# Two transformer layers on one core: the stores of the results are asked for by ScalarE's queue instead of SyncE's

## The reference

```python
def _L0_cond_ref(x, t_emb, W_ada, b_ada, Wq, Wkd, Wku, Wvu, Wo):
    ...
    scores = jnp.where(mask[None, None], jnp.asarray(-jnp.inf, x.dtype), scores)
    attn = jax.nn.softmax(scores, axis=-1)
    y = jnp.einsum('bhts,bhsd->bhtd', attn, v_exp)
    out = y.transpose(0, 2, 1, 3).reshape(B, T, C) @ Wo.T
    return x + out
def _L1_cond_ref(x, pos_ids, time_emb, ln1_w, ln1_tw, ln2_w, ln2_tw, Wq, Wk, Wv, Wo, Wg, Wu, Wd):
    ...
    x = res + ctx @ Wo.T
    res = x
    h = ada_rms(x, time_emb, ln2_w, ln2_tw)
    mlp = jax.nn.silu(h @ Wg.T) * (h @ Wu.T) @ Wd.T
    return res + mlp
```

## Time and profile before

| what | us |
|---|---|
| median of three executions | 1815.69 |
| the profiled execution | 1816.14 |
| its span | 1814.2 |
| PE busy | 1713.0 |
| DVE busy | 1155.3 |
| ACT busy | 945.1 |
| POOL busy | 398.2 |

### The profile page before, as it was taken

How to read it: one execution, slowest core, us unless ns; L and a number is a source line. 1 busy time by engine, 2 the same in 40 slices (tenths; PEclk the granted TensorE clock), 3 DMA queues, 4 the chain that set the end, 5 groups by cost and what they waited for, 6 DMA issues and landing times.

```text
span 1814.2 us, 37803 instructions
## 1 busy us (share of the span) xinstructions
PE 1713.0 (94%) x12416; PEld 929.7 (51%) x12416; DVE 1155.3 (64%) x2956; ACT 945.1 (52%) x2775; POOL 398.2 (22%) x554
## 2 busy tenths in 40 slices
PE   6586888999999999999999999999999999999999
PEld 2244444565455545555455554555455554555444
DVE  6768566585677657685576756676576855767320
ACT  3836456364664537554483646645385644835320
POOL 3448477011110211111110111111121111101120
PEclk9786999999999999999999999999999999999999
DMA  7867489472794448662594637843495626936220
GB/s 244 149 183 117 126 187 241 102 129 74 157 187 88 83 111 186 139 115 80 126 193 91 119 84 163 172 96 76 120 191 124 122 73 139 194 88 108 99 70 23
DMA packets 527236, 234.38 MB, mean 129 GB/s; under 512 B 476336, under 2 KB 493744, under 8 KB 527024
## 3 DMA queue, kind: packets, MB, share of 16 engines
q1 hardware_dynamic: 511472, 175.09, 48.8%
q10 hardware_dynamic: 15552, 56.63, 9.9%
HBM read 90.09 MB, written 16.78 MB: 59 GB/s over the span
## 4 chain that ended last, share of the span: by engine, by line
PE 77%; DVE 9%; DMA 6%; issue 4%; ACT 3%; SPq 1%; DVEq 0%; POOL 0%; ACTq 0%
PE up L1395 8%; PE up L1397 8%; PE up L1396 8%; PE gate L1395 7%; PE gate L1397 7%; PE gate L1396 7%; DMA prob_t<-prob 5%; PE bank L1395 4%; PE y L1395 4%; PE y L1397 4%; PE bank L1396 4%; PE y L1396 4%; PE bank L1397 4%; PE bank L1422 2%; PE bank L1459 1%
## 5 line engine op out<-in xcount | busy, mean ns | idle before, releaser
L843 ACT ACTIVATE bank<-bank,low 128x128 f32<-128x128 f32 (+2 forms) x768 | 302.7, 395 | 63.4 <-DVE low L1079 36.7
L685 POOL TENSOR_TENSOR inner_t<-inner,inner_t 128x512 f16<-128x512 f32 x128 | 149.0, 1164 | 665.6 <-ACT inner_t L1022 665.6
L1086 DVE TENSOR_TENSOR prob<-bank,prob 128x512 f16<-128x512 f32 (+1 forms) x320 | 202.8, 634 | 57.1 <-ACT prob L852 55.9
L852 ACT ACTIVATE prob<-bank 128x512 f16<-128x512 f32 (+1 forms) x320 | 178.7, 558 | 75.4 <-DMA prob_t<-prob 52.7
L1395 PE MATMUL up<-mlp,ring 128*128 128x512 f16 x512 | 195.2, 381 | 13.3 <-DVE inner L1360 13.3
L1350 DVE SCALAR_TENSOR_TENSOR silu<-silu,gate 128x512 f32<-128x512 f32 x128 | 87.9, 687 | 181.4 <-ACT silu L1016 180.5
L1395 PE MATMUL gate<-mlp,ring 128*128 128x512 f16 x512 | 194.7, 380 | 1.4 <-DVE mlp L1055 0.9
L1397 PE MATMUL up<-mlp,ring 128*128 128x512 f16 x512 | 195.2, 381 | 0.0
L1396 PE MATMUL up<-mlp,ring 128*128 128x512 f16 x512 | 195.2, 381 | 0.0
L1396 PE MATMUL gate<-mlp,ring 128*128 128x512 f16 x512 | 194.5, 380 | 0.0
L1397 PE MATMUL gate<-mlp,ring 128*128 128x512 f16 x512 | 194.5, 380 | 0.0
(11 more groups left out here) (176 smaller groups left out, 4020.7 us busy)
## 6 DMA issues: line engine op xcount, KB each, us to landing
ring<-wgu_dram ACTq DMA_DIRECT2D x108, 512.0 KB, 3.8
x_in<-x_dram SPq DMA_DIRECT2D x18, 512.0 KB, 3.8
x_res<-x_mid SPq DMA_DIRECT2D x16, 512.0 KB, 4.9
wgu_dram<-ring SPq DMA_DIRECT2D x16, 512.0 KB, 3.6
out_dram<-x_res SPq DMA_DIRECT2D x32, 256.0 KB, 2.4
prob_t<-prob SPq DMA_TRANSPOSE x256, 3.6
inner_t<-wd_t_dram SPq DMA_DIRECT2D x4, 1024.0 KB, 8.7
ring<-wg_t_dram SPq DMA_DIRECT2D x16, 256.0 KB, 4.0
```

What stands on the lines that cost most here:

```text
L685: pool.tensor_tensor(inner_t[:, 1, f, :], inner[:], inner_t[:, 0, f, :], ALU.subtract).then_inc(inner_low, 1)
L843: ins = act.activation(bank_[:, at:at + wid], bank_[:, at:at + wid], ACT.Exp, bias=low[:, j % BANKS, k:k + 1], scale=-1.0, accum_out=total)
L852: act.activation(terms(prob[:, g % SLOTS, 0, :], layer, j), terms(work_bank[USE[f"unit{layer}", j] % BANKS][:], layer, j), ACT.Copy).then_ ...
L1086: dve.tensor_tensor(terms(prob[:, slot, 1, :], layer, j), terms(work_bank[USE[name] % BANKS][:], layer, j), terms(prob[:, slot, 0, :], lay ...
```

## The change

`store` moves from SP's stream to ACT's. SP keeps the transpositions, the loads of x, the residual copies and, at the end of a round, its wait for the four stores. On ACT a store stands at the end of the step in which the tile is summed (`behind`), after that step's exponentials and before the next unit's `prob_highs`. The stores of the last pair, after the MLP that is done alone, go to the end of ACT's stream.

```diff
             def round_(n, m, first=False, last=False):
                 residual(m)
...
                         need_apart(sp, table_made, count(n, 1, 1), (cond_used, 1))
                         load_pos((n[0], n[1] + (not last)))
-                    store(m, step)
                 need_apart(sp, out_stored, count(m, 16 * DT, 16 * DT), (cond_used, 1))
...
             round_((None, NP - 1), (None, NP - 2), last=True)
             residual((None, NP - 1))
-            for step, _ in PLAN:
-                store((None, NP - 1), step)
             sp.wait_ge(out_stored, NP * 16 * DT)
...
                         if not first:
                             ring_loads(m, chunks_at(step, 4))
+                        store(m, step)
...
+            def store(n, step):
+                for t in tiles_at(step):
+                    s, tile = divmod(t, TILES)
+                    need_apart(act, d_read, count(n, DT, DT + t + 1), (cond_used, 1))
+                    act.dma_start(out_dram[sequence(n, s)][:, tile, :],
+                                 x_res[:, s, tile, :]).then_inc(out_stored, 16)
...
                 ring_loads((None, NP - 1), [f], last=True)
+            for step, _ in PLAN:
+                store((None, NP - 1), step)
```

More of the change, by code:

```diff
@@ L550, in residual @@
                     sp.dma_start(x_res[:, s], x_mid[:, s]).then_inc(res_copied[s], 16)
[L552 to L557, removed]
             def turn_probs(n, layer, j):
```

## The result

The changed kernel takes 1824.68 us (median of 5 runs, 1821.23 to 1827.0), the kernel before 1814.99 us in the 5 runs beside it. The ratio is 1.0053 with an interval of 1.0038 to 1.0068: slower, by 6.9 to 12.3 us. The forecast was 1812.0 us with a range up to 1817.4, and is wrong in size and in sign. The profiled execution took 1821.23 us, the shortest of the five, against 1816.14 before; spans 1819.4 and 1814.2 us.

The account below looks back on a forecast made before the run. PE was taken to bound the kernel, busy 94% of the span. Less waiting at line 1430 saved 3.7 us, the other terms zero, so the median went from 1815.7 to 1812.0 us; range for all 1809.6 to 1817.4.

Parts of the forecast that it names:

- the one on ACT at `end`: Tile 3's store before ACT's first activations: up to 0.36 us delay, covered by PE's MLP parts; costed at zero.
- unit 7's landing: Transposition at `unit1_7`: without the store behind it lands in 3.1 or 4.8 us, cutting PE's line 1430 waits by 3.7 us.
- the bad unit 13: Unit 13's transposition landing in 4.8 us beside a code packet; all rounds like it gave the lower bound, 2.0 us.
- unit 13's good rounds: Unit 13's transposition landing near 3.1 us, three of six rounds; the forecast gave unit 7 this in half its rounds.
- The sum: PE's six waits at line 1430: three rounds freeing 0.95 us, three 0.5, less 0.7, giving 3.7 us saved.
- The first (only issue time is saved): Rival at units 7 and 8: unit 7 still lands in 5.3 us, total 1815.7 us; chance 0.32.
- The second, contention on ACT's queue: Rival at unit 7: the store on ACT's queue slows its landing, 4.5 us more, 1820.2 us; chance 0.11.
- The third: Rival on ACT: store instructions delay high halves or a round's start, up to 2.5 us, 1817.5 us; chance 0.07.
- From the end of unit 7's issue to unit 8's: Gap on SP between these transpositions: from 0.90 us to about 0.23, so unit 8 starts 0.67 us earlier.
- ACT's high half of unit 8: After tile 1's store on ACT: begins at most 0.4 us later against DVE's sum, covered by DVE; costed at zero.
- The last store: At the kernel's very end, moved from SP to ACT behind the same wait: zero, or 0.1 us either way.
- The rule of the Trainium skill: For stores moved between queues: issuing engines share 16 DMA engines, only issue time is saved; sum zero against 3.7 us.

Follow-up runs that it names:

- experiment 1: Changed kernel with tile 3's store back on SP, tiles 0 to 2 still on ACT: 1814.81 us, ratio 0.9994 to the kernel before.
- experiment 2: Kernel before with only tile 3's store moved to ACT, SP keeping tiles 0 to 2: 1822.68 us, ratio 1.0037.
- experiment 3: Kernel before, all stores on SP, ACT given only the wait for tile 3's sum at step end: 1821.1 us, ratio 1.0036.
- experiment 4: Kernel before, all stores on SP, ACT waiting at step end for tile 2's sum, made long before: 1817.57 us, ratio 1.0004.
- experiment 5: Changed kernel, all stores on ACT, with ACT's loop written out so no branch ends a round: 1814.66 us, ratio 0.9996 to the kernel before.
- experiment 6: Changed kernel with tile 3's store asked for on ACT in the next round, at step fill0.1: 1817.56 us, ratio 1.001 to the kernel before.
- experiment 7: Kernel before, all stores on SP, tile 1's asked for at unit1_12 instead of unit1_7: 1815.89 us, ratio 0.999.
- experiment 8: As experiment 7, plus five met waits on SP between units 7 and 8, in the loop's five rounds: 1814.34 us, ratio 0.999.

## Why the prediction was wrong

**The step that failed** is the one on ACT at `end`, in the words of the prediction: "a delay of up to 0.36 us of the first activations is covered by the MLP parts that PE has in that step", costed at zero with a bound of 2.5 us. It counted the store's instructions and not what they hold up. The wait is met late, at 843.86, while in the kernel before ACT's sequencer had passed that place at 840.55 and gone on to the jump. The delay is not 0.36 us but 3.5, and what PE feels of it is 7.3 us in five rounds. The rows were there to be read: the sum of tile 3 ends at 843.45, after ACT's sine at 843.12, and ACT next waited only 0.74 us. I asked what the activations wait for and not what the sequencer does between them. Experiments 1 to 5 show that this carries the loss: the kernels in which the jump is covered or gone are within 0.1% of the kernel before.

**Mis-sized: unit 7's landing.** The term was 3.7 us, with 2.0 as its lower bound ("every round like the bad unit 13"). PE's wait at line 1430 fell by 1.5 us as printed (1.1 to 1.8 in experiments 1 and 5 to 8), so it came out a little below the bound. And no gain in time was measured: the kernels with the shorter wait and no exposed jump (experiments 1 and 5 to 8) have ratios of 0.999 to 1.001, none of them clear of 1. Every round is like the bad unit 13: 4.5 to 4.9 us in the changed kernel, and the same with no store at all. What the store behind it adds is 0.4 to 0.9 us, round by round, in four rounds of six. That part of the reading of the earlier trace rows was right. The step from unit 13's good rounds to unit 7 was not: half of the 3.7 us rested on taking one unit as a model of another. The sum also took every round but one as a landing of 5.3 us with a wait of 0.95; the round at 804 us lands in 4.53 as well, and PE's waits in these first two rounds are only 0.55 and 0.23 us.

**The rivals.** The first (only issue time is saved) is nearest for unit 7, though the landing did move by half a microsecond. The second, contention on ACT's queue, didn't happen at unit 7: the store is asked for 1.6 us ahead of it and lands in 2.6 us, and unit 7 lands sooner than before and not later. The measured loss lies nearest to this rival's 1820.2 us, but by another cause. The third named the right place, the start of a round, with a price per round of 0.36 us where 1.5 was paid, and a total of 1817.5. None of the three has a wait that holds the sequencer.

**What was right.** From the end of unit 7's issue to unit 8's is 0.23 us on SP, as forecast; they follow each other at 1.46 us (2.13 before). ACT's high half of unit 8 starts at 1015.84, 2.39 us later in time than before, and DVE's low half 2.35 us later: nothing is held up there. The last store costs nothing: from it to the end of the span it is 2.4 us in both kernels.

**The rule of the Trainium skill** that was weighed ahead (page "DMA: Bandwidth & Descriptors", section "Issuing engines are not separate DMA queues") gave a sum of zero, and the kernels with stores on ACT in which no jump is exposed (experiments 1, 5 and 6) come out at 0.9994, 0.9996 and 1.001: in time the runs agree with that rule. That section says nothing of the wait that comes along. The Trainium skill, page "Advanced Engine Details and Errata", section "Control Flow Timing", gives about 51 ns for a branch that is always taken and about 108 ns for a compare-and-branch. ACT's loop branch is a compare-and-branch, and its record is 0.04 to 0.06 us long here; the measurement decides. The 2.7 to 3.0 us behind it aren't in that section.

**Open.** What the 2.7 to 3.0 us of the jump consist of was not tested; the packet of code seen in them is the nearest lead. What makes unit 13 land in 3.1 us in some rounds, and unit 7 never where there is a packet, stays open; both meet a packet of the instruction queue 2.0 to 3.1 us behind their issue in nearly every round. The median grew by 9.7 us where the profiled execution, the shortest of five, grew by 5.1; the rows' 6.4 us is near the latter. Printed waits and spans agree only to a few us: in experiment 1 the waits sum to 2.6 us more than before, and the span is 2.2 us shorter.

## What to carry to other kernels

A transfer that moves to a compute engine brings its wait with it, and the wait stops that engine's sequencer at that place. Look at how far the sequencer runs ahead there and what stands next in its program. Here a loop's branch stood next and cost 0.4 to 0.5% of the time, while the waits at the three other places cost nothing that could be measured. The test is cheap: leave the transfer where it was and put only the wait in.

## What the runs showed of the hardware

Where ACT's loop branch is taken, the first instruction of the next round is read 2.4 to 3.0 us behind it (45 records in nine kernels). The time shows as idle where nothing is queued: 2.7 to 3.0 us (15 of the records, in three kernels, the chain's "2.94 issue" and "2.95 issue" among them). Where nothing is queued and the branch isn't taken, at the loop's last round, it is 0.03 us. Each of the 45 has an 8 KB packet of the instruction queue q14 that starts 0.9 to 1.2 us behind the branch. Not every engine is like that: in the kernels before and after, SP and POOL read on 0.2 to 0.3 us behind a branch that is taken.

Unit 7's transposition of 128 x 512 lands in 3.1 to 3.5 us in the round near 380 us, where no packet of the instruction queue q8 starts while it is under way. In the later rounds one packet of 0.02 MB starts 2.0 to 2.8 us behind its issue, and it lands in 4.5 to 5.0 us (36 rounds in six kernels). With a store behind it as well it lands in 5.2 to 5.4 us in 14 of 24 rounds (the kernel before and experiments 2, 3 and 4), and in 4.5 to 4.8 us in the other ten. The packet alone doesn't settle it: over all ten kernels unit 13 lands in 3.0 to 3.3 us beside such a packet in about a third of its rounds.
